# Moving chunk loads between spreading transfers, six result places for the output tiles, and step 1's exponentials among the norms

## The reference

```python
q, k, v = proj(wq, bq), proj(wk, bk), proj(wv, bv)     # x @ w.T + b, 16 heads of 32
scores = jnp.einsum('bhqd,bhkd->bhqk', q, k) / scale
probs = jax.nn.softmax(scores, axis=-1)
ctx = jnp.einsum('bhqk,bhkd->bhqd', probs, v)
x = _layernorm(x + (ctx @ wo.T + bo), axis=-1)
x = _layernorm(x + _L0_ffn_ref(x, ...), axis=-1)       # 8 experts, top 2, and a shared one
```

## Time and profile before

| | us |
|---|---|
| median of 3 runs | 2333.41 (2331.19 to 2333.7) |
| the profiled execution | 2339.22 |
| its span, first to last instruction | 2337.4 |
| TensorE busy | 2142.5 (92%) |
| GpSimd busy | 1098.9 (47%) |
| ScalarE busy | 853.4 (37%) |

### The profile page before, as it was taken

One profiled execution on the slowest core, in us unless ns is written; L12 is line 12 of the kernel. 1 busy time (PEld: TensorE's weight loads), 2 busy tenths in 40 slices (PEclk: granted clock), 3 DMA queues, 4 the chain that ended last, 5 costly groups with the idle time before them and its releaser, 6 DMA issues. The chain is left out here.

```text
span 2337.4 us, 34373 instructions
## 1 busy us (share of the span) xinstructions
PE 2142.5 (92%) x9524; PEld 1183.9 (51%) x9525; DVE 1125.9 (48%) x2041; ACT 853.4 (37%) x1508; POOL 1098.9 (47%) x1054
## 2 busy tenths in 40 slices
PE   7999899899899899899999998781799999999997
PEld 5544445445445445445554433461554444445886
DVE  6766564466555466465366622450222222223875
ACT  2355453355454255454255563320111111111332
POOL 1366664566765465766356675327111111111651
PEclk9999999999999999899999999895899999999999
DMA  4231333221333212332302302560132222223762
GB/s 135 64 70 44 76 69 91 75 64 29 92 69 90 80 37 53 91 74 56 113 15 65 69 11 86 203 262 9 42 104 90 90 90 90 89 85 118 218 188 77
DMA packets 96849, 202.82 MB, mean 87 GB/s; under 512 B 26912, under 2 KB 27424, under 8 KB 94752
## 3 DMA queue, kind: packets, MB, share of 16 engines
q1 hardware_dynamic: 83744, 165.04, 24.2%
q0 software_dynamic: 12928, 35.70, 5.6%
HBM read 110.68 MB, written 39.13 MB: 64 GB/s over the span
## 5 line engine op out<-in xcount | busy, mean ns | idle before, releaser
L757 DVE TENSOR_REDUCE max_half<-ps_side 128x1 f32<-128x512 f32 x1024 | 664.0, 685 | 432.5 <-PE ps_side L527 421.7
L464 POOL TENSOR_TENSOR acc<-probs 128x512 f32<-128x512 f32 x512 | 640.8, 1281 | 387.2 <-ACT probs L675 387.2
L675 ACT ACTIVATE probs<-ps_s 128x512 f32<-128x512 f32 x1024 | 574.1, 597 | 494.6 <-PE ps_s L544 431.6
L544 PE MATMUL ps_s<-kq_stack 97*128 97x512 f32 x1024 | 464.5, 457 | 35.0 <-ACT probs L675 27.4
L527 PE MATMUL ps_side<-kq_stack 96*128 96x512 f32 x1024 | 402.5, 404 | 6.9 <-DVE res L815 3.1
L544 PEld LDWEIGHTS ps_s<-kq_stack 97*128 97x128 f32 x1024 | 194.4, 191 | 373.1 <-ACT probs L675 228.1
L555 PE MATMUL ps_ctx<-probs,v_sb 128*32 128x512 f32 x2048 | 276.1, 612 | 0.0
L1425 PE MATMUL ps_gu<-gu_sb,xT_e 128*128 x576 | 261.2, 596 | 0.4 <-issue 0.3
L1323 POOL DMA_INDIRECT x_g<-x,who_all x72 | 68.2, 948 | 393.4 <-PE ps_t L1415 325.1
L527 PEld LDWEIGHTS ps_side<-kq_stack 96*128 96x128 f32 x1024 | 197.5, 193 | 42.1 <-DVE max_half L757 7.8
L1425 PEld LDWEIGHTS ps_gu<-gu_sb,xT_e 128*128 128x128 f32 x576 | 103.7, 190 | 107.5 <-issue 107.3
(11 more groups left out here) (190 smaller groups left out, 2369.7 us busy)
## 6 DMA issues: line engine op xcount, KB each, us to landing
kq_stack<-kq SPq DMA_DIRECT2D x192, 256.0 KB, 5.0
y_slots<-y_t SPq DMA_DIRECT2D x72, 256.0 KB, 2.3
res<-inv_rows SPq DMA_DIRECT2D x128, 64.0 KB, 2.0
probs<-x SPq DMA_DIRECT2D x16, 512.0 KB, 5.7
x<-res SPq DMA_DIRECT2D x32, 256.0 KB, 2.0
x_r<-x SPq DMA_DIRECT2D x32, 256.0 KB, 3.8
x_t<-x SPq DMA_DIRECT2D x32, 256.0 KB
gu_sb<-wgu SPq DMA_DIRECT2D x8, 1024.0 KB, 14.7
```

The source lines that it names most:

```text
L464: nc.gpsimd.tensor_tensor(acc[:, h, :], probs[:, (loc - 1) % 2, h, :] if j == 1 else acc[:, h, :], probs[:, loc % 2, h, :], ALU.add).then_ ...
L544: nc.tensor.matmul(ps_s[:, (loc * HG + h) % RING, :], k_stack[par][0:3 * HD + 1, h, kt * P:(kt + 1) * P], q_stack[par][0:3 * HD + 1, h, ha ...
L675: nc.scalar.activation(probs[:, loc % 2, h, :], ps_s[:, (loc * HG + h) % RING, :], ACT.Exp, scale=HD ** -0.5).then_inc(probs_ready, 1)
L757: nc.vector.reduce_max(max_half[:, u // 2, u % 2:u % 2 + 1], bank, AX.X).then_inc(side_free, 1)
```

## The change

Four things change, all in attention. The number of matmuls, exponentials and transfers stays.

- `load_x` for chunks 2 and 3 moves on SyncE's queue: from behind all twelve spreading transfers to behind head 1's (chunk 2) and behind head 2's (chunk 3). Chunks 0 and 1 stand ahead of the spreading in both kernels.
- Output tiles 2 to 5 are kept in `x_nat` slots 0 to 3 instead of in `res`, so a batch has six result places; `stats`, `mv` and the like have eight. Line 815 waits for a store only at tiles 6 and 7, and for those of tiles 0 and 1. As those slots are `probs` of even steps, the exponential of step 0, head h, now waits until tile h + 2 is stored.
- The four exponentials of step 1 stand among the norms, no longer at the start of the next batch.
- TensorE's wait on all eight evacuations of the tail at the first slot of a batch is split over the first three slots.

```diff
-EXPS_BETWEEN = {3: (0, 1), 4: (2,), 5: (3,)}
+EXPS_BETWEEN = {3: ((0, 0), (0, 1)), 4: ((0, 2),), 5: ((0, 3), (1, 0), (1, 1)), 6: ((1, 2),), 7: ((1, 3),)}
...
+        x2_out = [sem(f"x2_out{t}") for t in range(KT)]
+
+        def res_of(t):
+
+            return x_nat[:, t - 2, :] if 2 <= t < 6 else res[:, t % 2, :]
...
                         sp.dma_start(kq_stack[par][r * HD:(r + 1) * HD, :, h, :].bitcast(F32),
                                      kq[h * HD:(h + 1) * HD, parts, :].bitcast(F32)).then_inc(stacked[h], 16)
+                    if h in between:
+                        between[h]()
...
                 if not (last and g >= G - 2):
-                    spread(m + 2, g % 2, m)
-                if x_chunks:
-                    load_x(b + 1, m + 3, range(2, 4))
+                    spread(m + 2, g % 2, m, {h: lambda i=h + 1: load_x(b + 1, m + 3, [i])
+                                             for h in (1, 2)} if x_chunks else {})
...
-                        if loc == 0 and slot == 0:
-                            pe.wait_ge(tail_free, b * TAIL + KT)
+                        if loc == 0 and slot < SIDE_RING:
+                            pe.wait_ge(tail_free, b * TAIL + KT - (2 - slot if slot < 2 else 0) - (slot < 2))
...
-                elif h == 0:
-                    act.wait_ge(tail_free, b * TAIL + KT // 2 * (loc + 1))
+                else:
+                    if h == 0:
+                        act.wait_ge(tail_free, b * TAIL + KT // 2 * (loc + 1))
+                    if loc == 0:
+                        act.wait_ge(x2_out[h + 2], 16 * (b + 1))
...
-                        if loc + 1 < BSTEPS:
+                        if 1 <= loc < BSTEPS - 1:
                             exps(b, loc + 1, slot)
...
-                    for h in EXPS_BETWEEN.get(t, ()):
-                        exps(b + 1, 0, h)
+                    for loc, h in EXPS_BETWEEN.get(t, ()):
+                        exps(b + 1, loc, h)
...
-                dve.wait_ge(x2_out[s], 16 * (b * (KT // 2) + t // 2 + 1))
+                if t >= 6:
+                    dve.wait_ge(x2_out[t - 6], 16 * (b + 2))
```

More of the change, by code:

```diff
@@ L142, in attention @@
         inv_few = sb("inv_few", [P, HALF // HD])
-        stats = sb("stats", [P, 2, 6])
-        mv = sb("mv", [P, 2, 2])
-        var_eps = sb("var_eps", [P, 2, 1])
+        stats = sb("stats", [P, KT, 6])
+        mv = sb("mv", [P, KT, 2])
+        var_eps = sb("var_eps", [P, KT, 1])
         minus_half = sb("minus_half", [P, 1])
-        rstd = sb("rstd", [P, 2, 1])
-        minus_mean = sb("minus_mean", [P, 2, 1])
-        shift = sb("shift", [P, 2, 1])
+        rstd = sb("rstd", [P, KT, 1])
+        minus_mean = sb("minus_mean", [P, KT, 1])
+        shift = sb("shift", [P, KT, 1])
         ps_s = ctx.enter_context(nc.psum_tensor("ps_s", [P, RING, HALF], F32))
@@ L199, in attention @@
         x2_ready = sem("x2_ready")
-        x2_out = [sem("x2_out0"), sem("x2_out1")]
+        x2_out = [sem(f"x2_out{t}") for t in range(KT)]
+        def res_of(t):
+            return x_nat[:, t - 2, :] if 2 <= t < 6 else res[:, t % 2, :]
         block = ctx.enter_context(nc.Block())
@@ L264, in load_x, with spread @@
                                      "a p t -> (a p) t")).then_inc(x_in[i % 2], 16)
-            def spread(n, par, m=None):
+            def spread(n, par, m=None, between={}):
                 sp.wait_ge(proj_free, PROJ * (n + 1))
@@ L308, in body @@
                 if g == 0:
-                    sp.wait_ge(x2_out[1], 16 * (b * (KT // 2) + 1))
+                    sp.wait_ge(x2_out[7], 16 * (b + 1))
                     sp.sem_inc(passed_sp, 1)
@@ L346, in store @@
                 sp.dma_start(x2[bass.ds(b, 1), t * P:(t + 1) * P, :].rearrange("a p d -> (a p) d"),
-                             res[:, t % 2, :]).then_inc(x2_out[t % 2], 16)
-            for i in range(2):
-                sp.sem_inc(x2_out[i], 16)
+                             res_of(t)).then_inc(x2_out[t], 16)
+            for t in range(KT):
+                sp.sem_inc(x2_out[t], 16)
             sp.dma_start(first_w(0), wkqT[0]).then_inc(x_first[0], 16)
@@ L375, in _ @@
             tail(B - 1, True)
-            for i in range(2):
-                sp.wait_ge(x2_out[i], 16 * (B * KT // 2 + 1))
+            for t in range(KT):
+                sp.wait_ge(x2_out[t], 16 * (B + 1))
         @block.gpsimd
@@ L435, in add_bo @@
                     if t >= 1:
-                        s = (t - 1) % 2
+                        s = t - 1
                         pool.wait_ge(var_made, b * KT + t)
@@ L688, in take @@
                 else:
-                    act.wait_ge(x2_out[0], 16 * (b * (KT // 2) + 1))
+                    act.wait_ge(x2_out[6], 16 * (b + 1))
                 nc.scalar.activation(rsum, ps_sum[:], ACT.Identity).then_inc(sum_taken, 1)
             def norm(b, t):
-                s = t % 2
                 act.wait_ge(rstd_made, 2 * (b * KT + t + 1))
-                nc.scalar.activation(res[:, s, :], res[:, s, :], ACT.Identity, bias=shift[:, s, :],
-                                     scale=rstd[:, s, :]).then_inc(x2_ready, 1)
+                nc.scalar.activation(res_of(t), res_of(t), ACT.Identity, bias=shift[:, t, :],
+                                     scale=rstd[:, t, :]).then_inc(x2_ready, 1)
             def batch(b, last):
@@ L723, in _ @@
                     side_unit(-1, -1, *what)
-            for h in range(HG):
-                exps(0, 0, h)
+            for loc in range(2):
+                for h in range(HG):
+                    exps(0, loc, h)
             with act.Fori(0, B - 1) as b:
@@ L811, in o_tile @@
                 dve.wait_ge(xbias, k + 1)
-                dve.wait_ge(x2_out[s], 16 * (b * (KT // 2) + t // 2 + 1))
+                if t >= 6:
+                    dve.wait_ge(x2_out[t - 6], 16 * (b + 2))
                 if t == 1:
                     dve.wait_ge(ctx_done, (b + 1) * G * NHALF)
-                nc.vector.tensor_tensor(res[:, s, :], bank, x_nat[:, t, :], ALU.add).then_inc(tail_free, 1)
+                nc.vector.tensor_tensor(res_of(t), bank, x_nat[:, t, :], ALU.add).then_inc(tail_free, 1)
                 dve.wait_ge(tail_free, u + 1)
-                nc.vector.bn_stats(stats[:, s, :], res[:, s, :]).then_inc(ln_chain, 1)
+                nc.vector.bn_stats(stats[:, t, :], res_of(t)).then_inc(ln_chain, 1)
                 dve.wait_ge(const_in, CONSTS)
                 dve.wait_ge(ln_chain, k + 1)
-                nc.vector.bn_aggr(mv[:, s, :], stats[:, s, :]).then_inc(aggr_made, 1)
+                nc.vector.bn_aggr(mv[:, t, :], stats[:, t, :]).then_inc(aggr_made, 1)
                 dve.wait_ge(aggr_made, k + 1)
-                nc.vector.tensor_scalar(minus_mean[:, s, :], mv[:, s, 0:1], -1.0, None, ALU.mult)
-                nc.vector.tensor_scalar(var_eps[:, s, :], mv[:, s, 1:2], EPS, None, ALU.add).then_inc(var_made, 1)
+                nc.vector.tensor_scalar(minus_mean[:, t, :], mv[:, t, 0:1], -1.0, None, ALU.mult)
+                nc.vector.tensor_scalar(var_eps[:, t, :], mv[:, t, 1:2], EPS, None, ALU.add).then_inc(var_made, 1)
             dve.wait_ge(w_high, 2)
```

## The result

The changed kernel takes 2311.59 us in the median of 4 runs (2305.03 to 2316.1), the kernel before 2333.55 us: a ratio of 0.9904, 95% interval 0.9878 to 0.993, some 22 us less. A second measurement beside other runs gave 0.9895 (0.9873 to 0.9916). Forecast were 2307 us, in a range of 2297 to 2319.

A forecast was written before the change was run, and what follows sets the result against it. TensorE, busy 92% of the span, was taken as the bound, so its idle stretches and the slow clock after them count. 15.8 + 10.7 = 26.5 us off 2339.2 gives 2312.7; 5.8 over the median, so 2307 us, range 2297 to 2319.

The forecast's parts named there:

- The chunks: Group 2's projections: chunk 2's wait goes, about 3 us of wait stands at chunk 6; 15.8 us gained over three batches.
- The landing of the moved loads: Chunks 2 and 3 on SyncE's queue: each lands 3.9 us after issue, chunk 3 at 243.2.
- the first of my own signs of being wrong: Group 2: the prediction is wrong if GpSimd's fold behind chunk 3 starts later than 246.
- The other two signs: Wrong if ScalarE ends the wait at the change of batch, or a new wait stands at step 3 of group 2.
- The clock: Group 2, behind the wait for chunk 6: falls to half in two of three batches, 3.3 us each, 6.6 us lost.
- The rival built on it: Group 2: the moved chunk lands in its own 2.7 us, not by its place among the spreading; 2304 us, chance 0.10.
- The change of batch: Between batches: VectorE's return, not ScalarE's, bounds TensorE; 3.5, 3.6 and 4.2 us, less 1.4, plus 0.8 for clock: 10.7 us.
- The stores: Step 0's exponentials wait for tiles 2 to 5, 2.0 us median; hidden, 2 us ahead of VectorE's return.
- The slower rival: Change of batch: stores of 8 us delay the exponentials, costing about 8 us each; about 2342 us, chance 0.03.
- The sum: Whole kernel: 15.8 us from chunks plus 10.7 from changes of batch, 26.5 us off.

The follow-up runs named there:

- two places: Changed kernel with two result places again, step 1's exponentials still among the norms: 2316.82 us, 0.9914 of the kernel before.
- four early: Changed kernel with chunks 2 and 3 loaded behind head 1's spreading, chunks 4 and 5 behind head 3's, ahead of the row of maxima: 2303.04 us, ratio 0.9856.
- both chunks behind head 1: Changed kernel with chunk 3's load right behind chunk 2's, after head 1's spreading transfers: 2250.88 us on a faster chip, 0.9873 of the kernel before.
- VectorE straight: Changed kernel with VectorE's loop written out, the other engines' loops left: 2250.98 us on a faster chip, 0.988 of the kernel before.
- chunks alone: Kernel before with only the loads of chunks 2 and 3 moved between the spreading transfers: 2324.42 us, ratio 0.9949.
- straight and both chunks: Changed kernel with VectorE, ScalarE and GpSimd loops written out and chunks 2 and 3 loaded behind head 1: 2231.39 us on a faster chip, ratio 0.9793.

## Why the prediction was right

**The chunks: the mechanism right, the size off by 3.3 us (15.8 forecast, 12.5 measured).** Chunk 2 was there in time and its wait went, GpSimd was the bound from chunk 3 on, and the wait for chunk 6 came, 2.35, 1.56 and 2.33 us in the three batches where I had said 3. The second profile of the changed kernel has 14.7 us and the one with two places 15.7, so part of the 3.3 us is the clock of one execution. Three terms were mis-sized. *The landing of the moved loads:* I took 3.9 us from loads that stood at the end of the traffic; between the spreading transfers they take 5.0 and 5.6 us in batch 0, about what the neighbours take, 5.0 us in the median by the page of the kernel before. I had taken the operation's own row at another place where the neighbours' row was the nearer one. SyncE was some 0.9 us ahead of my account, so GpSimd's fold behind chunk 3 started 10.9 us into the stretch, where I had 10.0 and the kernel before 15.1. That is past the first of my own signs of being wrong (246 us, which is 10.7 into the stretch) by 0.1 us: the landing was wrong by more than I had allowed for. The other two signs did not come: no wait stands at step 3 of group 2 in the changed kernel, and ScalarE does not end the wait at the change of batch. *A wait for chunk 3*, 1.00, 1.90 and 1.13 us, was not in my account of TensorE; with the wait for chunk 6 it makes 3.4 us in each batch, near the 3 us forecast in one place. *The clock:* it fell behind the wait for chunk 6 in all three batches, where I took two of three, and once behind that for chunk 3, but at some 1.7 us a time, 3.0 in batch 2, where I had 3.3 (TensorE's busy time of 28.78, 30.39 and 30.05 us with one, two and one longer fall, against 27.0 at full clock in four early). The runs with both chunks behind head 1 and with four early show the rest of it: the landing of chunk 3 was worth moving, and it paid clearly once chunk 4's load moved too (95.8 us, then 91.9).

**The fixed cost from the Trainium skill** (DMA: Bandwidth & Descriptors, Anatomy of one DMA), by which a chunk would land after an estimated 2.6 us, does not hold for these loads among the spreading, which took 5.0 and 5.6 us; on a quiet queue 2.7 us were measured, near it. The rival built on it fell.

**The change of batch: right, and 3.4 us better than sized (10.7 forecast, 14.1 measured).** The next wait was the one named, the unit in place 3 for VectorE's return from the branch, and in the run with VectorE straight it is gone. From the last projection piece, VectorE was back after 66.5 us where before it was 67.7 (440.56 less 374.06; 443.35 less 375.63): 1.2 us sooner instead of 0.4. The last addition started 0.4 us sooner, as forecast; the aggregation behind the last statistics started another 0.35 us sooner, and the gap of the branch was 0.4 us shorter, neither of which I had foreseen or can explain. That VectorE has the longest branch, as I had written, does not hold in general: at the first change of batch in the changed kernel ScalarE's and GpSimd's take 3.2 us from the branch to the next instruction and VectorE's 2.7, and VectorE was the bound because TensorE needed its result first. The clock made the rest: I took off 1.4 us for half clock running on, and it lasted shorter than before (mean clock of these stretches 0.98, 0.98 and 1.00 against 0.94, 0.94 and 0.96). With two result places it is 0.96, 0.96 and 1.00, and TensorE is busy 1.1 to 1.2 us longer at each looped change: some 2.4 of the 5.2 us that the places are worth there are the clock.

**The stores.** The new wait of step 0's exponentials on the stores hid, as forecast, with 3 us to spare where I had said 2. The slower rival had no part in it.

**The sum** came out at 26.6 us against 26.5, by two errors that cancel, which is luck. The median shows 22 us. The prologue, up to the first pieces of batch 0, took 2.0 us longer than in the one profile of before, and the expert half 1.7 us; the code of neither changed, other runs of this study scatter by as much (the prologue with chunks alone was 3.0 us longer), and I put it down to the choice of execution without having shown it.

## What to carry to other kernels

When a transfer is moved in among others, price its landing by its new neighbours, not by its own record at its old place. A load that is brought forward pays only as far as the next wait on the consumer's queue: look for that one before sizing the gain, here chunk 4's load behind the row of maxima. At a loop's end, put work whose results others wait for ahead of the branch on every engine, or write the loop out if the program is small enough.

## What the runs showed of the hardware

A loop's branch that is taken holds VectorE, ScalarE, GpSimd and SyncE up for 2.5 to 3.4 us, from the branch to the next instruction, in the traces of the kernel before and the changed one; where the loop is left, it is 0.05 us or less on ScalarE and GpSimd in the kernel before. TensorE shows no such gap: in the changed kernel its branch stands at 428.2 us, and its last output tiles are multiplied until 435.6. The only sign of a branch in the profile is "issue", 2.81 us of it on VectorE in the changed kernel, and on GpSimd:

```profile
441.98 4.97 POOL L469 TENSOR_TENSOR acc<-probs 128x512 f32<-128x512 f32 x4 [3.33 <-issue]
```

The Trainium skill says that a taken branch breaks the sequential fetch of instructions (Runtime: NRT & Kernel Launch, Instruction fetch mechanics); the trace agrees as far as the delay goes, for at the third change of batch, which goes straight on, VectorE works on without a gap in the kernel before and waits 0.34 us, for TensorE, in the changed one:

```profile
1140.33 2.48 DVE L765 TENSOR_REDUCE max_half<-ps_side 128x1 f32<-128x512 f32 x4 [0.34 <-PE ps_side L532]
```

What I had not expected is that writing loops out sped up the steps too, by about 1.2 us in 72 for each group. It came with VectorE, ScalarE and GpSimd written out, and not with VectorE alone, and TensorE's and SyncE's loops added nothing. Whether ScalarE or GpSimd is enough, and whether the semaphore counts that a loop computes in registers are the cause, was not tried.

The length of a wait alone did not decide whether TensorE's clock fell to half. Behind waits of 1.55 or 1.56 us for chunk 6 it fell in one batch of three in the kernel before and in two of three with four chunks early. It fell behind most waits of 2.2 to 2.6 us, yet it stayed up behind 2.33 us with VectorE straight and behind 2.62 us in straight and both chunks, both in batch 2; the stretch of the latter:

```profile
914.95:944.76 29.81, 27.05 (x141) 13.56 (x140) 16.16 (x26) 13.54 (x26) 25.88 (x24) 1.00 0.45 117
```
